# A three-stage sequence model on one core: one decay exponential, one pair of head products and two ending steps moved in the first stage's turn

## What is computed

```
zxbcdt = u @ W_in.T                      # z, x B C, dt
dt  = softplus(zxbcdt[..., -4:] + dt_bias)
xBC = silu(causal_conv4(xBC) + conv_b)   # x, B, C
L   = exp(segsum(A * dt))                # decay of each head
Y   = einsum(C, B, L, x * dt)            # (C B^T * L) (x dt)
y   = (Y + x * D) * silu(z)
y   = y * rsqrt(mean(y * y) + 1e-5) * norm_w
out = y @ W_out.T
```

## Time and profile before

| | |
|---|---|
| median of 3 runs | 2573.65 us (2569.4 to 2577.73) |
| profiled execution | 2572.47 us |
| its span, first to last instruction | 2570.7 us |
| TensorE busy | 2137.3 us, 83% |
| VectorE busy | 1982.9 us, 77% |
| ScalarE busy | 1824.7 us, 71% |
| GpSimd busy | 1528.5 us, 59% |
| mean granted TensorE clock | 0.955 of full speed |

### The profile page before, as it was taken

How to read it: one execution, slowest core, us unless ns; L and a number is a source line. 1 busy time by engine, 2 the same in 40 slices (tenths; PEclk the granted TensorE clock), 3 DMA queues, 4 the chain that set the end, 5 groups by cost and what they waited for, 6 DMA issues and landing times. The chain is left out here.

```text
span 2570.7 us, 46195 instructions
## 1 busy us (share of the span) xinstructions
PE 2137.3 (83%) x13308; PEld 1102.2 (43%) x13308; DVE 1982.9 (77%) x5418; ACT 1824.7 (71%) x4730; POOL 1528.5 (59%) x1364
## 2 busy tenths in 40 slices
PE   6888789999999998567667667767899999999997
PEld 3555455555555554122222222222455555555553
DVE  5776687777777776399998999998877777777774
ACT  3444587787776877487778778876778777777784
POOL 2333466565665554277877777777766556655562
PEclk8999899999999999779989998998999999999999
DMA  3000000000000000000000000000000000000000
GB/s 133 1 0 1 12 10 14 14 9 18 10 14 14 9 14 10 1 0 1 1 1 1 1 1 0 0 1 4 14 14 10 14 13 10 18 14 22 17 14 17
DMA packets 12353, 30.04 MB, mean 12 GB/s; under 512 B 2256, under 2 KB 2256, under 8 KB 11728
## 3 DMA queue, kind: packets, MB, share of 16 engines
q1 hardware_dynamic: 12112, 27.41, 4.0%
HBM read 8.52 MB, written 2.10 MB: 4 GB/s over the span
## 5 line engine op out<-in xcount | busy, mean ns | idle before, releaser
L521 POOL TENSOR_TENSOR arena<-arena 128x512 f32<-128x512 f32 x256 | 325.7, 1272 | 482.7 <-DVE arena L1661 482.7
L588 POOL TENSOR_TENSOR arena<-arena 128x512 f32<-128x512 f32 x256 | 331.2, 1308 | 138.8 <-ACT arena L1349 134.0
L527 POOL TENSOR_TENSOR arena<-arena,SR 128x512 f32<-128x512 f32 x256 | 272.5, 1064 | 83.0 <-ACT SR L1200 82.4
L1759 DVE TENSOR_TENSOR_SCAN arena<-arena,psum 128x512 f32<-128x512 f32 x256 | 310.9, 1214 | 3.4
L984 PE MATMUL psum<-BS,tabs 96*128 96x512 bf16 x384 | 137.1, 413 | 205.3 <-DVE arena L1759 203.7
L534 POOL TENSOR_TENSOR P<-P,RS 128x512 f32<-128x512 f32 x256 | 270.3, 1056 | 36.2 <-DVE RS L1535 35.5
L1052 PE MATMUL psum<-arena,first 128*128 128x512 f32 x512 | 281.6, 640 | 2.5 <-POOL arena L581 2.3
L867 PE MATMUL psum<-rest,HA 128*128 128x512 f32 x512 | 266.6, 603 | 2.3 <-DVE arena L1404 1.5
L1667 DVE TENSOR_REDUCE SM<-arena 128x8 f32<-128x512 f32 x256 | 174.4, 681 | 87.4 <-ACT arena L1190 74.5
L984 PEld LDWEIGHTS psum<-BS,tabs 96*128 96x128 bf16 x384 | 35.8, 100 | 402.0 <-DVE arena L1759 364.7
L1165 ACT ACTIVATE P<-P,NB 128x128 f32<-128x128 f32 x512 | 200.3, 391 | 9.7 <-issue 8.8
(11 more groups left out here) (224 smaller groups left out, 5280.1 us busy)
## 6 DMA issues: line engine op xcount, KB each, us to landing
arena<-arena SPq DMA_DIRECT2D x128, 128.0 KB, 2.3
rest<-in_rest SPq DMA_DIRECT2D x1, 4183.0 KB, 20.7
out<-X SPq DMA_DIRECT2D x8, 256.0 KB, 2.3
X<-in_x SPq DMA_DIRECT2D x1, 1536.0 KB, 11.5
tabs<-in_tabs SPq DMA_DIRECT2D x1, 1216.0 KB, 8.3
first<-in_first SPq DMA_DIRECT2D x1, 875.5 KB, 4.5
X<-in_x SPq DMA_DIRECT2D x1, 512.0 KB, 5.8
```

Source lines behind the costliest of these rows:

```text
L521: nc.gpsimd.tensor_tensor(CQ[:, n % 2, :], CQ[:, n % 2, :], SQN[:, n % 2, :], ALU.add).then_inc(f_rope, 1)
L527: nc.gpsimd.tensor_tensor(heads, heads, SR[:, n % 2, :].unsqueeze(2).to_broadcast([128, HEADS, DH]), ALU.mult).then_inc(f_qk, 1)
L588: nc.gpsimd.tensor_tensor(WU[:, k % DEEP, :], RG[:, k % DEEP, :], U[(t.j + pair) % 2][:, k % 2, :], ALU.mult).then_inc(m_wu, 1)
L1759: v.tensor_tensor_scan(HS[:, k % DEEP, :], AB[:, k % DEEP, :], B_BANK[k % 2], 0.0, ALU.mult, ALU.add).then_inc(m_hs, 1)
```

## The change

Three steps of the first stage's turn are written at other places; nothing is added or taken away.

1. ScalarE: the silu session goes from step 12 to step 14. Exponential 8 is written ahead of the session in step 14, so it now precedes it.
2. TensorE: `heads_out(3)` goes from behind step 15 to the head of step 14, ahead of the transposes and of the norm's variance (step 14).
3. VectorE: the ending's steps 0 and 1 go from behind the first and ahead of the second product to the very head of the turn, ahead of `x_times_dt`.

```diff
--- before.py
+++ after.py
@@ -734,6 +734,8 @@
                             segsum(t, h // 2 + 1)
                     if t.before:
                         a_pe_ending(t, h)
+                    if t.states and h == 14:
+                        heads_out(t, 3)
                     if t.after:
                         a_pe_beginning(t, h)
                     if t.ahead:
@@ -742,8 +744,6 @@
                         a_pe_final(t, h)
                     if t.states and h in (5, 9, 13):
                         heads_out(t, h // 4 - 1)
-                if t.states:
-                    heads_out(t, 3)
 
 
             def wait_scores(k, m, g):
@@ -1125,7 +1125,7 @@
                 elif h == 6:
                     t.wait_ge(a_spd, 2, 2, pair=1)
                     A(sp[:, 4, :], sp[:, 3, :], ACT.Ln).then_inc(a_sp, 1)
-                elif h == 12:
+                elif h == 14:
                     for k in range(2):
                         t.wait_ge(a_cx, 8, 4 * k + 4, pair=1)
                         A(XA[side][:, k, :], XA[side][:, k, :], ACT.Silu, bias=F("a_convb", k, k + 1)).then_inc(a_act, 1)
@@ -1496,6 +1496,9 @@
                     conv_bc(t, (2, 3))
 
             def a_dve_turn(t):
+                if t.before:
+                    a_dve_ending(t, 0)
+                    a_dve_ending(t, 1)
                 for h in range(16):
                     if t.states and h == 0:
                         x_times_dt(t)
@@ -1509,7 +1512,7 @@
                         t.wait_ge(a_lm, 8, q + 1)
                         t.wait_ge(a_y, 8, q - 3)
                         TT(MM[:, q % 4, :], LM[:, q % 2, :], CBM[:, q // 4, :], ALU.mult).then_inc(a_mm, 1)
-                    if t.before:
+                    if t.before and h > 1:
                         a_dve_ending(t, h)
                     if t.after and h:
                         a_dve_beginning(t, h)
```

## The result

The changed kernel took 2590.95 us, the median of 5 runs (2579.43 to 2596.36), beside 2577.28 for the kernel before, measured with it: a ratio of 1.0049, with an interval of 1.0031 to 1.0067. It is slower by half a per cent. The forecast was +12.6 us on the kernel before, or +0.49%, and the ratio is that; 2590.95 itself lies 6 us above the 2585 forecast and inside the range.

A forecast was written before the change was run, and what follows sets the result against it. In the first stage's turn, TensorE's chain from the transposes to L686 would set the convolution's start, VectorE the rest. +6.2 - 5.8 + 13.2 - 1 = +12.6 us on the profiled 2572.47 gave 2585.1, forecast 2585, range 2571 to 2593.

The forecast's parts named there:

- The session's delay: ScalarE: exponential 8 waits for the last segment sum, so the session comes 3.29 us later, c_times_b(0) on TensorE 1.47 later.
- heads_out(3) and the ending in the idle time: TensorE's heads_out(3) hides in the wait for the session; VectorE's 3.03 us of ending steps at the turn's head are free.
- The convolution, +1.04 us a turn: VectorE's convolution waits for TensorE's L686 and starts at 193.33 instead of 192.29 us, 6.2 us over 6 turns.
- The clock, 6 x 2.2 = +13.2: TensorE's gathered 3.05 us wait drops the clock to 1.2 GHz, costing 2.2 us a turn, bounds 0 and 3.4.
- Given back, -5.8: L721's wait on TensorE shrinks by 0.43 us, so the falls that lengthen three turns go: -5.8 us, bounds 0 and -5.8.
- The last turn, -1: heads_out(3)'s 1.80 us wait in the last turn goes, the later session takes part back: between -1.8 and 0, taken as -1.
- The rest of the kernel: Beyond the first stage, some 270 us, nothing was counted; time lost outside it would show the forecast wrong.
- The clock holds: Rival: TensorE's gathered idle time brings no costly clock fall; sum -0.6 us, 2572 us; chance 0.33.
- The session isn't delayed: Rival: exponential 8's sum is complete when exponential 7 ends, session slips only 0.51 us; sum -17.2, 2555 us; chance 0.05.
- Every fall is double: Rival: half-width products and c_times_b keep TensorE's clock down, 3.4 us a turn; sum +19.8, 2592 us; chance 0.10.
- The rule that the prediction took from the Trainium skill: TensorE's gap to avoid is longer than this one; by it the clock would hold and its price be 0.

The follow-up runs named there:

- experiment 1: The changed kernel with 11 unused 128x128 matmuls behind heads_out(3), in TensorE's wait for the session: 2572.17 us, ratio 0.9988.
- experiment 2: The changed kernel with the eighth segment sum moved from step 12 to step 10 on TensorE: 2560.91 us, ratio 0.9945.
- experiment 4: The kernel before with only the silu session moved to step 14 behind exponential 8: 2598.12 us, ratio 1.0088.
- experiment 5: The changed kernel with the ending's two steps put back behind the turn's first product: 2593.34 us, ratio 1.0069.
- experiment 8: The changed kernel with the eighth segment sum at step 10 and the ending's two steps back behind the first product: 2567.03 us, ratio 0.9970.
- experiment 7: The changed kernel with the eighth segment sum at step 10 and unused matmuls behind heads_out(3), 4 a turn, 10 in pair 6's: 2556.77 us, ratio 0.9933.
- experiment 6: The kernel before with only the eighth segment sum moved from step 12 to step 10: 2577.72 us, ratio 1.0011.
- experiment 3: The changed kernel with the silu session back at step 12, exponential 8 behind it, the other two moves kept: 2590.53 us, ratio 1.0058.

## Why the prediction was right, and where it was not

The direction, the two delays and the clock's part in the loss were right, and experiments 1 and 2 show them. That the total agrees to a hundredth of a per cent is luck in part: the interval of the ratio reaches from 0.31 to 0.67%, and several terms below were off in both directions.

**The session's delay** (+3.29 us, and +1.47 for c_times_b(0)): right. The table load is 3.80 us behind the seventh exponential, the transposes 8.32 (8.32 forecast), c_times_b(0) 10.21 (10.17 forecast). Experiment 2 shows the cause by removing it.

**heads_out(3) and the ending in the idle time:** right. heads_out(3) starts 4.80 us behind the seventh exponential where 4.47 was worked out, which costs nothing, and only shortens the wait ahead of the transposes to 2.65 us, where "3.05" had been forecast.

**The convolution, +1.04 us a turn:** right, 16.83 us against 16.80. From there to the next exponential 7 it is 13.58 us and not 13.46, so a turn at full clock takes 30.4 and not 30.3 us: 0.1 a turn that I had left out. The first turn is longer by another 1.1 us, since its last segment sum comes later; that was not in the sum either.

**The clock, 6 x 2.2 = +13.2:** the step that failed in its form. I had expected "a granted clock of 0.50 behind them in nearly every turn" and at most 3.4 us for one turn. The profiled run has the fall in 2 of 6 turns; each lasts 10 us and costs 4.15 us, over the upper bound; the mean is 1.4 a turn. By the measured totals it is more: 15.7 to 18.8 us between the change and experiment 1, less the 2.9 by which experiment 1's last turn is shorter, are 2.1 to 2.7 a turn, if nothing else differed. So the price lies between 1.4 and 2.7, and the 2.2 was near as a product of two numbers that I had both wrong in the profiled run, how often and how long: that is luck. The upper bound was taken from one fall of 3.4 us. What makes a fall longer is not shown; in experiment 4, too, c_times_b's 16-row products come behind the waits, and most falls last 6.8 us.

**Given back, -5.8:** right in that the falls behind L721 go, but not in the step that led there. L721's wait was to shrink by 0.43 us because TensorE is later; it shrank by 0.97 where it had been 2.39, to 1.42. In experiment 4 the session is late too and the wait stays at 2.38. Experiments 5 and 8 bring wait and fall back by undoing the ending's move: it is this move, costed as "free", that takes the wait away.

**The last turn, -1:** mis-sized. From its seventh exponential to the stage's end it takes 30.50 us (30.57 before), since the clock falls there too (253 to 260 us). In experiment 1, at full clock, it takes 27.62 (237.85 to 265.47). So the fall takes 2.9 us; what the step would be worth with the clock of before was not measured apart.

**The rest of the kernel:** I had put it at nothing, as it has no changed instruction. From the last exponential to the end it takes 2303.9 us before, 2300.9 in the change and 2308.4 in experiment 1. Over all ten kernels' profiles it ranges from 2300.9 (the change) to 2308.5 us (experiment 8). These are single profiles, and why they differ was not looked into; a difference of a few us between two totals need not come from the first stage. It explains why the profiled span grew by 6.9 us only where the stage grew by 9.9: the forecast holds for the medians, and on the profiled pair alone it would look too high. It also means that part of the 11.5 us between the change's profiled and its median run may lie outside the stage.

**The rivals.** "The clock holds" gave 2572 us from turns of 30.3: experiment 1, which makes the clock hold, gives 2572.17 from turns of 30.4. "The session isn't delayed" gave 2555: experiment 2 makes its condition nearly real (a load 0.90 later instead of 0.51) and gives 2560.91, experiment 7 with the clock kept 2556.77. The working of both stands; what the change lacks is their conditions. "Every fall is double" (6.8 us) did not come: single falls lasted longer, 10 us here and 12.9 us in experiment 2, but not every turn had one.

The rule that the prediction took from the Trainium skill (TensorE: Matmul & The Clock Gate, "HAM oscillation — how this bites in real kernels") would have kept the clock up for a gap of 2.7 us. The trace disagrees behind three of the seven sessions of the profiled run (waits of 2.66, 2.66 and 2.96 us, each with a fall), and agrees behind the other four (2.65 to 2.77 us, without one).

Still open: what decides, for one and the same wait of 2.65 us, whether the clock falls (159.34 no, 189.75 yes, in one run). The runs of the change spread over 17 us, and only one has a profile, so how many falls the others had is not known. No kernel moved the waits in time to test it.

## What to carry to other kernels

Before a step is put ahead of a block on its engine, look when its input is complete on the engine that feeds it; if that is later, move the producer too, or the whole block inherits the wait. Here the same move costs 0.5% without the producer and gains 0.55% with it, and the producer's move alone gains nothing. A wait into which an engine's idle time is gathered has to be priced twice on TensorE, by its length and by the clock behind it; where it can't be removed, unused matmuls in it took 11.3 us off the stage in the profiled runs (15.7 us of the whole by the ratios) and delayed nothing.

## What the runs showed of the chip that was not expected

- The same wait can be followed by a fall or not, in one execution: after 2.65 us at 159.34 L704 took 0.66 us, after 2.66 us at 189.75 it took 1.11. L721's wait of 2.38 to 2.39 us had a fall behind it in the kernel before and in experiments 5, 6 and 8, and none in experiment 4. The long waits of experiments 3 and 4, six of 3.83 to 4.77 us and seven of 4.26 us, all had one.
- Once at 1.2 GHz, TensorE stayed there for 10 us with 8.95 us of matmuls in them, and for 12.9 us with 12.62 us in experiment 2, where the earlier trace rows has 3.4 us.
- The switch to silu costs ScalarE no more than the table load of 1.28 us in the sessions looked at: the next instruction started 1.29 us behind the load's start in experiment 2 (167.38 and 168.67), 1.30 in the change (185.23 and 186.53).
